# Order of small steps at the attention's ends and inside the graph layers

## The reference, cut to what matters

```python
h = jnp.maximum(_layernorm(x, axis=-1), 0.0)
x = x + _L0_gnn_ref(h, batch0, edge_index, edge_attr_16, ..., 32)
h = jnp.maximum(_layernorm(x, axis=-1), 0.0)
x = x + _L1_gnn_ref(h, edge_index, L1_gnn_W1, L1_gnn_b1, L1_gnn_W2, L1_gnn_b2, L1_gnn_W3, L1_gnn_b3)
h = jnp.maximum(_layernorm(x, axis=-1), 0.0)
x = x + _L2_gnn_ref(h, edge_index, L2_gnn_W, L2_gnn_b)
h = jnp.maximum(_layernorm(x, axis=-1), 0.0)
x = x + _L3_gnn_ref(h, L3_gnn_weight, edge_weight, edge_index)
# a layer: h @ W, then segment_sum(msg, col), norm = dis[row] * dis[col]; L2 and L3 end in a relu
```

## Time and profile before

| what | value |
|---|---|
| median of 3 runs | 1504.21 us (1503.85 to 1505.04) |
| the profiled execution | 1502.93 us |
| its span, first to last instruction | 1501.7 us |
| mean granted TensorE clock | 0.973 of full |
| PE busy | 1408.0 us (94%) |
| DVE, ACT busy | 937.0 us, 557.2 us |

### The profile page before, as it was taken

How to read it: one execution, slowest core, us unless ns; L and a number is a source line. 1 busy time by engine, 2 the same in 40 slices (tenths; PEclk the granted TensorE clock), 3 DMA queues, 4 the chain that set the end, 5 groups by cost and what they waited for, 6 DMA issues and landing times.

```text
span 1501.7 us, 22184 instructions
## 1 busy us (share of the span) xinstructions
PE 1408.0 (94%) x8974; PEld 851.9 (57%) x8974; DVE 937.0 (62%) x1450; ACT 557.2 (37%) x965; POOL 89.0 (6%) x79
## 2 busy tenths in 40 slices
PE   6569999999998799899999999999999999799998
PEld 6458888788887566444444444454444444344444
DVE  7879989899998688567745673533245222442322
ACT  1146655565554345731124111411234222332322
POOL 4001100110000121000000100001200000000000
PEclk9779999999999899999999999999999999899999
DMA  7233343335334572300000100003211222534201
GB/s 286 70 128 115 130 142 109 111 105 180 126 121 146 194 248 102 92 1 29 1 1 0 57 1 0 1 1 97 65 36 57 56 70 57 210 136 141 102 0 56
DMA packets 67664, 134.42 MB, mean 90 GB/s; under 512 B 9442, under 2 KB 21858, under 8 KB 66020
## 3 DMA queue, kind: packets, MB, share of 16 engines
q1 hardware_dynamic: 65444, 122.84, 24.3%
q0 software_dynamic: 1280, 5.77, 1.4%
q10 hardware_dynamic: 832, 4.33, 0.7%
HBM read 79.61 MB, written 53.31 MB: 89 GB/s over the span
## 4 chain that ended last, share of the span: by engine, by line
PE 75%; DVE 13%; ACT 4%; issue 3%; DMA 0%; SPq 0%; ACTq 0%; DVEq 0%
PE banks L1900 26%; PE banks L1859 13%; PE banks L1962 11%; PE banks L959 6%; PE banks L944 6%; PE banks L1297 3%; DVE x_sb L693 2%; PE banks L964 2%; PE banks L937 2%; DVE x_sb L682 1%; PE banks L1802 1%; PE banks L910 1%; DVE fields L661 1%; DVE dis L2174 1%; DVE count_max L2175 1%
## 5 line engine op out<-in xcount | busy, mean ns | idle before, releaser
L1900 PE MATMUL banks<-g,count 128*128 128x512 f16 x1024 | 229.3, 381 | 0.5 <-DVE tiles L2144 0.5
L1900 PE MATMUL banks<-count,g 128*128 128x512 f16 x1024 | 225.4, 381 | 0.0
L1859 PE MATMUL banks<-w_parts,h_parts 128*128 128x512 f16 x960 | 216.1, 383 | 5.0 <-issue 3.7
L1900 PEld LDWEIGHTS banks<-count,g 128*128 128x128 f16 x1024 | 100.0, 98 | 119.3 <-issue 2.3
L1962 PE MATMUL banks<-g,part 128*128 128x512 f16 x768 | 165.9, 379 | 0.0
L1900 PEld LDWEIGHTS banks<-g,count 128*128 128x128 f16 x1024 | 100.2, 98 | 114.7 <-issue 2.2
L1859 PEld LDWEIGHTS banks<-w_parts,h_parts 128*128 128x128 f16 x960 | 91.0, 98 | 125.0 <-issue 14.4
L693 DVE TENSOR_TENSOR x_sb<-eb_parts,x_sb 128x4096 f16<-128x4096 f16 x64 | 146.3, 2285 | 0.0
L959 PE MATMUL banks<-x_sb 128*128 128x256 f16 x1024 | 125.6, 277 | 8.2 <-DVE bias L703 6.0
L1962 PEld LDWEIGHTS banks<-g,part 128*128 128x128 f16 x768 | 75.1, 98 | 90.6
L959 PEld LDWEIGHTS banks<-x_sb 128*128 128x128 f16 x1024 | 100.9, 99 | 30.5 <-DVE x_sb L693 7.7
(11 more groups left out here) (295 smaller groups left out, 1953.2 us busy)
## 6 DMA issues: line engine op xcount, KB each, us to landing
weight_dram<-w_new SPq DMA_DIRECT2D x62, 256.0 KB, 2.4
count<-weight_dram SPq DMA_DIRECT2D x29, 512.0 KB, 7.2
qk_dram<-stage SPq DMA_DIRECT2D x64, 128.0 KB, 1.9
tiles<-x_dram SPq DMA_DIRECT2D x32, 256.0 KB, 3.5
x_dram<-tiles SPq DMA_DIRECT2D x32, 256.0 KB, 2.8
count<-in_x SPq DMA_DIRECT2D x4, 1024.0 KB, 10.9
h<-in_x SPq DMA_DIRECT2D x16, 256.0 KB, 3.7
h_dram<-h_t SPq DMA_DIRECT2D x8, 512.0 KB, 2.9
```

The source lines that it names most:

```text
L1859: mm = pe.matmul(out, m.h_parts[:, slot, zh, k], m.w_parts[:, zw, k], start=n == 0 and layer != 3, stop=n == len(passes) - 1)
L1900: mm = pe.matmul(m.agg_ps[:, b], lhs, rhs, start=i == 0 and z == 0, stop=i == NT - 1 and z == 1)
```

## The change

Some steps take other places in the lists; one function is called earlier or later on each engine. In the attention, the degree rows move to later periods, and `root` and `norm` of the last three tiles move into layer 0's products. In layer 0 and layer 4, the splits are issued one step ahead, and in layer 0 the transposes stand behind a product instead of ahead. In the sums, the places n of `peak_row` and `peak_all` change, and so do those of the transposes in layer 3's last quarter. The first two tiles of layer 4 are split inside layer 3's sums, the last tile of h is turned behind product 1, and the first raw part is made at tile 8 of products(4).

```diff
-DEGREES = {-4: (0, 1), -3: (2,), -2: (3,)}
+DEGREES = {-4: (0,), -3: (1,), -2: (2, 3)}
...
-    root(slice(SHORT, NT), 2)
+
+    def last_root():
+        root(slice(SHORT, NT), 2)
+    tools.last_root = last_root
...
-    norm(slice(SHORT, NT), 2)
+
+    def last_norm():
+        norm(slice(SHORT, NT), 2)
+    tools.last_norm = last_norm
...
-            act.wait_ge(s["copied"], 3 * NT)
+            act.wait_ge(s["copied"], 3 * NT - PER + t // PER + 1)
...
+            if layer in (0, 4) and 2 <= t + 1 < NT:
+                split_hi(layer, t + 1)
             if t < NT:
-                if layer == 0:
-                    pair = t // 2 + 2 + t % 2
-                    if pair < NT // 2:
-                        for u in (2 * pair, 2 * pair + 1):
-                            if t % 2 == 0:
-                                copy_turned(0, u)
-                            else:
-                                relu(0, u)
...
-                if t >= 2 or layer == 4:
+                if t >= 2 and layer not in (0, 4):
                     split_hi(layer, t)
             if t >= late:
                 product_hi(layer, t - late)
+            if layer == 0 and t and t // 2 + 2 < NT // 2:
+                for u in (t // 2 * 2 + 4, t // 2 * 2 + 5):
+                    if t % 2 == 1:
+                        copy_turned(0, u)
+                    else:
+                        relu(0, u)
+            if layer == 0 and t == 2:
+                tools.last_root()
+            if layer == 4 and t == 1:
+                copy_turned(2, NT - 1)
+            if layer == 4 and t == 8:
+                act.wait_ge(s["e_scaled"], 1)
+                part_hi(0)
...
                 if c == GROUPS - 1:
+                    if b == PER - 1:
+                        copy_turned(2, t - 1)
                     act.wait_ge(s["var_last"], b + 1)
                     act.sqrt(m.rstd_last[:, b:b + 1], m.rstd_last[:, b:b + 1]).then_inc(s["std_last"], 1)
                     relu(2, t)
-                    copy_turned(2, t)
+                    if b in (1, 2):
+                        copy_turned(2, t - 1)
+                    if b == 1:
+                        split_hi(4, 0)
+                        split_hi(4, 1)
...
-            if n == len(passes) - 2 and t + 1 < NT and layer not in (0, 3):
+            if n == len(passes) - 2 and t + 1 < NT and layer not in (0, 3) and (layer, t) != (4, 1):
                 await_parts(layer, t + 1)
...
-                pair = t // 2 + 2
-                if layer == 0 and t % 2 == 0 and pair < NT // 2:
-                    turn(0, 2 * pair)
-                    turn(0, 2 * pair + 1)
...
-                if t > 1 and layer in (0, 3):
+                if t > 1 and layer in (0, 3) or (layer, t) == (4, 3):
                     await_parts(layer, t - 1)
                 product(layer, t - 1)
+                pair = t // 2 + 2
+                if layer == 0 and t % 2 == 1 and pair < NT // 2:
+                    turn(0, 2 * pair)
+                    turn(0, 2 * pair + 1)
+                if layer == 4 and t == 2:
+                    turn(2, NT - 1)
...
-            if n == 15:
+            if n == (17 if layer == 2 else 23):
                 peak_row()
-            if n == 20:
+            if n == (21 if layer == 2 else 28):
                 peak_all()
...
         elif layer < 2:
-            if n == 13:
+            if n == (22 if c == 1 else 13):
                 peak_row()
-            if n == 19:
+            if n == (28 if c == 1 else 19):
                 peak_all()
-        elif n in (20, 26, 32, 38):
-            turn(layer - 1, (c - 1) * PER + (n - 20) // 6)
-        if layer == 3 and c == GROUPS - 1 and n in (44, 54, 63):
-            turn(2, c * PER + (n - 44) // 9)
+        else:
+            before = (14, 18, 22, 26) if layer == 3 and c == GROUPS - 1 else (20, 26, 32, 38)
+            if n in before:
+                turn(layer - 1, (c - 1) * PER + before.index(n))
+        own = (46, 57, 63)
+        if layer == 3 and c == GROUPS - 1 and n in own:
+            turn(2, c * PER + own.index(n))
...
-    turn(2, NT - 1)
     products(4)
...
-            if t < NT and (t >= (3 if layer in (1, 2) else 2) or layer == 4):
+            if layer in (0, 4):
+                if 2 <= t + 1 < NT:
+                    split_lo(layer, t + 1)
+            elif t < NT and t >= (3 if layer < 3 else 2):
                 split_lo(layer, t)
+            if layer == 0 and t == 4:
+                tools.last_norm()
...
+            if layer == 4 and t == 8:
+                split_raw(0)
...
+                if b == 1:
+                    split_lo(4, 0)
+                    split_lo(4, 1)
...
-    split_raw(0)
     products(4)
```

More of the change, by code:

```diff
@@ L1765, in layers_act @@
         sums(layer)
-    act.wait_ge(s["e_scaled"], 1)
-    part_hi(0)
     products(4)
```

## The result

| | before | after |
|---|---|---|
| median | 1504.21 us | 1491.26 us |
| profiled execution | 1502.93 us | 1491.26 us |
| its span | 1501.7 us | 1490.0 us |
| mean granted clock | 0.973 | 0.978 |

The ratio of the times is 0.9907, 95% interval [0.9892, 0.9922]: 0.9% faster. The change of the medians is -12.95 us and that of the profiled spans -11.7 us, where the sum said -15.2; 1491.26 lies inside the forecast's range. One of the five executions of the changed kernel took 2102.24 us at a mean granted clock of 0.652; it is left out of the comparisons, and no profile shows where its clock was low.

A forecast was written before the change was run, and what follows sets the result against it. TensorE (PE), its instruction stream with its waits and half clock, was taken as the bound. The terms summed to -15.2 us: 1502.93 gives 1487.7, and the median, 1.3 higher, gives 1489.0 us, range 1483 to 1494.

The forecast's parts named there:

- attention's start: Between the scores of tiles 0 and 1: one degree row instead of two starts DVE earlier, gain 1.0 us, bounds 0 and 1.9.
- attention's end, layer 0's products: After the transposes of tiles 2 and 3: products start without waiting for tile 4's relu, gain 6.3 us, bounds 3.6 and 7.
- maxima, layer 0: Layer 0's sums: PE stalls 2.35 us at the second peak_row and 2.7 at the third, where one 2.8 stood; loss 2.2.
- half clock behind the four waits: Sums of layers 0 and 1: two of four stalls followed by half clock at 1.7 us each, loss 3.4, bounds 0 and 6.8.
- layer 3's last quarter, layer 4: Layer 3's sums end 3.9 us earlier, products 0 and 1 cover tile 15's chain; gain 14.4 us in all, bounds 9 and 15.5.
- rival that the maxima do not stall: Sums of layers 0 and 1: DVE has slack, so stalls and half clock go; -29 us, 1475 us, chance 0.10.
- rival of the long half clock: Layers 0 and 1: half clock behind new stalls lasts tens of us, slower than before; 40 us gives 1505, chance 0.02.
- Sixteen products at (1331.94 - 1288.66 - 1.5) / 16 = 2.61: Layer 4: each product takes 2.61 us, sixteen 41.8 us, from the old trace less half its stretch at half clock.
- second rival: Layers 0 and 4: ACT and DVE pace the products, waits of 0.3 us cost 2.4 + 4.2 = 6.6 us; 1495.5 us, chance 0.20.
- the sign of being wrong: Layer 4: the forecast is wrong if its products take over 2.7 us each.
- The 0.4 for `split_raw`: Layer 4's products at tile 8: part_hi and split_raw, now inside them, cost another 0.4 us on DVE.
- The 20.8 us by the starts: Ends of the attention and of layer 3: could give back 20.8 us by matmul starts, 15.1 by idle time alone.

The follow-up runs named there:

- the quarter back: Changed kernel with the transposes of tiles 8 to 11 in layer 3's last quarter back at steps 20 to 38: 1492.66 us, ratio 0.9916.
- the staggered ones: Changed kernel with peak_row at 11, then 17, 16, 15 (layer 2: 15, 19, then 25, 29), peak_all four steps behind each: 1474.98 us, 0.9806.

## Why the forecast was right, and where not

The terms of the sum against the two traces, by the starts of PE's matmuls (us, minus is faster):

| term | forecast | measured |
|---|---|---|
| attention's start | -1.0 | -1.2 in its stretch, and +1.8 ahead of it |
| half clock at 604.37 | none | +1.7 |
| attention's end, layer 0's products | -6.3 | -7.2 |
| maxima, layer 0 | +2.2 | +2.2 |
| maxima, layer 1, old half clock gone | +0.5 | +0.5 |
| half clock behind the four waits | +3.4 | +3.2 |
| layer 2 | +0.4 | +0.4 |
| layer 3's last quarter, layer 4 | -14.4 | -13.1 |
| sum | -15.2 | -11.7 |

**Right.** The waits at the maxima came at the places named, 2.36 and 2.65 us against 2.35 and 2.7, as did layer 2's 0.43. DVE's second maximum comes 3.5 us later after the sums' start than before (697.25 - 656.86 against 698.71 - 661.76), as the first one's place did (3.45). Putting back the first place alone took away the first wait of each pair and left the second, which is the mechanism of the forecast: DVE's chain hangs on the first `peak_row`, and the distance to the next one is the second limit. The rival that the maxima do not stall is refuted. The rival of the long half clock did not come in any profiled execution: each of the 14 half-clock stretches at waits in the sums of layers 0 and 1 lasted 3.41 us. That a wait of 3.6 us at the attention's end goes, that tile 12 is not waited for (transposed at 1266.93, relu at 1262.23), and that products 0 and 1 cover tile 15's chain, came as said. The next weights' load, now issued at 627.48, lands 10.6 us later and is first read at 658.78.

**Mis-sized: the product of layer 4.** The step was "Sixteen products at (1331.94 - 1288.66 - 1.5) / 16 = 2.61". That took the period of the old order for the new one. The period is set by a loop over ACT and DVE (PE's own twelve matmuls are 2.59 us), of 2.61 us before and 2.77 with the split first. With 13 periods it is 2.1 us; the hi part first in the changed kernel gave 1.8 of them back. The forecast named this as its second rival and as the sign of being wrong (over 2.7 us each), and it came for layer 4 at half the price given; in layer 0 the products do not wait at all. The 0.4 for `split_raw` did not show: the turn with it takes 2.77 us as well (1298.53 to 1301.30 on ACT).

**Mis-sized: layer 0's products.** A pair of products with two transposes takes 6.06 us (613.64 to 619.70), not the 6.18 of before. The 0.12 us stood between the transposes and the product (629.34 to 630.33 is 0.99 us, 618.82 to 619.70 is 0.88). With the ends it makes 0.9 us. The 20.8 us by the starts that the forecast names first is the 20.7 of its two terms, 6.3 and 14.4.

**Not foreseen: 3.5 us ahead of layer 0.** The degree rows gave 1.2 us: 1.7 from the missing row (forecast 1.85), less 0.5 for the scores in half clock (forecast about 1). But their stretch began 1.8 us later than before, at a place ahead of the whole diff, where all kernels run the same code. And the clock fell at 604.37, behind idle gaps of 1.05 and 0.36 us that the kernel before also has; there it fell at 612.36 instead, in the wait of 3.6 us. The ten kernels of the experiments have the same gaps there, and in none of their profiled executions did the clock fall behind them. So this 1.7 us seems part of an execution more than of the change. That the total came within 3.5 us of the sum is in part luck: these 3.5 and the 1.3 missed in layer 4 stand against 0.9, 0.2 and 0.2 on the other side, and the 1.8 and the 1.7 change from one execution to the next.

**The half clock was right as a mean only.** Over the nine profiled executions that wait at all, with the old places, the new ones or the first one back, waits of 2.2 to 2.7 us by brackets stood 26 times in the sums of layers 0 and 1, and 14 of them were followed by half clock: none of four with the old degree rows, two of four in the changed kernel, three of four with the quarter back. Equal code in these layers with equal waits gave 0 and 3.2 us, so that the forecast's two of four was met by luck. Nor does the length tell: it was 4 of 8 waits of 2.19 to 2.24 us, 4 of 10 of 2.48 to 2.52, and 6 of 8 of 2.62 to 2.67. What decides for a single wait is left open; no run here was made for it.

The two ends, the attention's and layer 3's, are each worth what the sum gave them within 1.3 us: 7.2 and 13.1 us alone, and the same together. The change's places for the maxima cost 5.1 us against those of before, and 14.2 against the staggered ones.

## What to carry to other kernels

A small step on PE that starts a chain on another engine belongs early, and the steps after it must lie as far apart as the chain is long (here 30.1 us from the first to the second, then 26.9). Moving the first one later to meet a late maximum delays the maximum too. When two operations of a loop swap places, measure the loop's period again; a period read from the old order need not hold. And give each wait of this length its share of half clock, here 14 of 26 times 1.6 us, but as a mean, since no single wait can be told.

## What the hardware showed that was not expected

A wait of 2.2 to 2.7 us (by brackets) was followed by 3.41 us at half clock in 14 of 26 cases, and at 604.37 two gaps of 1.05 and 0.36 us, 1.4 in all, were as well, in this kernel's profiled execution alone.

The gap before the second part of the first scores, in which PE waits for nothing that the profile shows, was 2.10 to 3.27 us in the twelve profiled kernels, whose code up to there is the same, and the part started within 3.9 us. The half clock about that place lasted 6.83 us in eight of them and 10.24 in four. A gain of 1.2 us in the attention can't be told from the times of two kernels.
